# An fp32 attention layer with a gated residual: the last head group's order of TensorE, ScalarE and VectorE work, and a result formed in two parts

## The reference

```python
xn = layernorm(x)
q, k, v = xn @ Wq.T, xn @ Wk.T, xn @ Wv.T       # 32, 8 and 8 heads of 128
q, k = rmsnorm(q, q_norm_w), rmsnorm(k, k_norm_w)
attn = softmax(q @ k.T / sqrt(128) + alibi_bias)  # causal, a slope for each head
s = (attn @ v) @ Wo.T
z = xn @ W.T + bias + sum_n(coef_n * (xn @ A_n.T) @ B_n.T)
out = x + s * (z * sigmoid(z))                    # x + s * silu(z)
```

## Time and profile before

| | us |
|---|---|
| median of 3 runs | 2694.29 |
| lowest, highest | 2690.87, 2695.27 |
| the profiled execution | 2691.18 |
| its span, first to last instruction | 2689.4 |
| TensorE busy in it | 2591.1 |
| GpSimd busy in it | 1705.5 |

### The profile page before, as it was taken

One profiled execution on the slowest core, in us unless ns is written; L12 is line 12 of the kernel. 1 busy time (PEld: TensorE's weight loads), 2 busy tenths in 40 slices (PEclk: granted clock), 3 DMA queues, 4 the chain that ended last, 5 costly groups with the idle time before them and its releaser, 6 DMA issues.

```text
span 2689.4 us, 39881 instructions
## 1 busy us (share of the span) xinstructions
PE 2591.1 (96%) x13840; PEld 2297.7 (85%) x13840; DVE 1648.2 (61%) x3530; ACT 1771.1 (66%) x4635; POOL 1705.5 (63%) x835
## 2 busy tenths in 40 slices
PE   5689999999999999999999999999999999999997
PEld 4578888888888888888888888888888888888886
DVE  6446566657667556566566666556666755655666
ACT  4366666666776667667767667666767666666763
POOL 3377877876667656656667656565666756655653
PEclk9899999999999999999999999999999999999999
DMA  7888788775445333433335433433334533333323
GB/s 259 269 269 281 240 266 263 256 259 190 128 145 174 109 119 100 154 111 104 110 106 183 133 117 104 154 105 106 112 108 136 180 110 106 118 110 118 111 69 129
DMA packets 179192, 418.45 MB, mean 156 GB/s; under 512 B 31152, under 2 KB 72240, under 8 KB 178096
## 3 DMA queue, kind: packets, MB, share of 16 engines
q1 hardware_dynamic: 177728, 414.78, 47.4%
q10 hardware_dynamic: 1264, 1.12, 0.1%
HBM read 343.48 MB, written 89.13 MB: 161 GB/s over the span
## 4 chain that ended last, share of the span: by engine, by line
PE 89%; DVE 3%; ACT 2%; DMA 2%; POOL 1%; issue 1%; SPq 1%; POOLq 0%; DVEq 0%; ACTq 0%
PE proj L486 21%; PE proj L488 21%; PE proj L487 21%; PE tr L581 5%; PE sc L486 3%; PE sc L487 3%; PE sc L488 3%; PE ot L487 3%; PE tr L561 3%; PE ot L488 3%; PE ot L486 3%; PE tr L554 1%; DMA wu<-xtok 1%; SPq L313 1%; DVE acc L1226 1%
## 5 line engine op out<-in xcount | busy, mean ns | idle before, releaser
L985 POOL TENSOR_TENSOR wl<-wl,wh 128x896 fp32r<-128x896 f32 x436 | 948.9, 2206 | 608.7 <-ACT wh L740 608.6
L486 PE MATMUL proj<-wh,xh 128*128 128x448 f32 x1792 | 673.8, 376 | 25.0 <-POOL wl L985 17.5
L487 PE MATMUL proj<-wl,xh 128*128 128x448 f32 x1792 | 661.1, 369 | 0.0
L488 PE MATMUL proj<-wh,xl 128*128 128x448 f32 x1792 | 661.1, 369 | 0.0
L996 POOL TENSOR_TENSOR wb_lo<-wb_lo,wb_hi 128x1024 fp32r<-128x1024 f32 x128 | 307.2, 2400 | 315.6 <-ACT wb_hi L750 315.6
L807 ACT ACTIVATE misc<-misc,negmax 128x128 f32<-128x128 f32 (+3 forms) x512 | 286.8, 565 | 250.2 <-DVE negmax L1202 250.2
L486 PE MATMUL proj<-o_hi,wb_hi 128*128 128x512 f32 x1024 | 424.9, 415 | 9.3 <-issue 6.1
L1226 DVE TENSOR_TENSOR acc<-acc,proj 128x512 f32<-128x512 f32 x480 | 327.7, 684 | 156.6 <-PE proj L488 155.3
L786 ACT ACTIVATE pT_hi<-tr 128x512 fp32r<-128x512 f32 (+3 forms) x512 | 197.3, 440 | 334.5 <-PE tr L581 334.5
L740 ACT ACTIVATE wh<-wl 128x896 fp32r<-128x896 f32 x436 | 395.5, 966 | 33.0 <-DMA wl<-wu 32.5
L488 PE MATMUL proj<-o_hi,wb_lo 128*128 128x512 f32 x1024 | 404.6, 395 | 0.0
(11 more groups left out here) (125 smaller groups left out, 4366.6 us busy)
## 6 DMA issues: line engine op xcount, KB each, us to landing
wl<-wu SPq DMA_DIRECT2D x436, 448.0 KB, 3.9
wb_lo<-wo_in SPq DMA_DIRECT2D x128, 512.0 KB, 3.3
wu<-xtok SPq DMA_DIRECT2D x13, 1792.0 KB, 10.2
wo_in<-wo SPq DMA_DIRECT2D x32, 512.0 KB, 6.0
xtok<-wa SPq DMA_DIRECT2D x52, 256.0 KB, 4.6
wu<-xtok SPq DMA_DIRECT2D x13, 896.0 KB, 5.6
gate_dram<-misc SPq DMA_DIRECT2D x32, 256.0 KB, 5.1
xtok<-xT SPq DMA_DIRECT2D x28, 256.0 KB, 5.1
```

Of the source, the lines that this page charges most:

```text
L486: pe.matmul(out, hi_l, hi_r, start=first, stop=False, skip_group_check=onto)
L487: pe.matmul(out, hi_l, lo_r, start=False, stop=False, skip_group_check=onto)
L488: return pe.matmul(out, lo_l, hi_r, start=False, stop=last, skip_group_check=onto)
L985: pool.tensor_tensor(w_slot(wl, w), w_slot(wl, w, True), w_slot(wh, w), ALU.subtract).then_inc(w_ready, 1)
```

## The change

Everything concerns the last group (n = 31) and what follows it.

- TensorE: for even v, `out_first` issues the first head's six matmuls (c = 0 into one bank, c = 1 into the other) before it waits for the second head, then the second head's six.
- ScalarE: `normalise` comes ahead of the copies of the turned queries, `split_b` behind three `probs_hi`.
- VectorE: `last_part` puts `add_out(v, 0)` first, and gives two of the four reciprocals to j = 0 and two to j = 1, one before and one behind the three `probs_lo`.
- GpSimd: `values_lo` ahead of `low_b` at j = 0.
- The result for c = 4 to 7: in the last step, once v = 125 is added, `base` forms acc x gate on VectorE and `add_base` adds it to x on GpSimd. After v = 127, `last_result` multiplies the bank of PSUM itself with the gate, with no `add_out`, and `finish` adds. The store of the gate and the loads of the second half come two steps earlier in SyncE's queue.

The core of the diff:

```diff
                         load_result(b, 0)
+                        store_gate(n)
+                        load_result(b, 1)
...
                     load_product(n + 2, P1)
                     load_product(n + 2, P2)
-                    store_gate(n)
+                    if n + 1 < NG:
+                        store_gate(n)
...
 
+            def out_head(v, c, hh, bank):
+                pair = v % 4 // 2
+                w = slice(hh * 512 + c * P, hh * 512 + c * P + P)
+                return three(bank[:], wb_hi[:, v % 2, w], wb_lo[:, v % 2, w],
+                             o_hi[:, pair, hh, :], o_lo[:, pair, hh, :], hh == 0, hh == 1)
...
+                out_head(v, c, 1, bank).then_inc(out_done, 1)
+
+            def out_first(v):
+
+                pe.wait_ge(wb_ready, v + 1)
+                pe.wait_ge(ot_free, v // 2 * 2 + 1)
+                banks = []
+                for c in range(2):
+                    banks.append(proj_bank(("o", v, c)))
+                    out_head(v, c, 0, banks[c])
+                pe.wait_ge(ot_free, v // 2 * 2 + 2)
+                for c in range(2):
+                    out_head(v, c, 1, banks[c]).then_inc(out_done, 1)
...
+                if n + 1 == NG and v % 2 == 0:
+                    out_first(v)
+                elif v >= 0:
...
-            for v in (NV - 2, NV - 1):
-                out_ready(v)
-                for c in range(4):
-                    out_proj(v, c)
+            out_first(NV - 2)
+            for c in range(2, 4):
+                out_proj(NV - 2, c)
+            out_ready(NV - 1)
+            for c in range(4):
+                out_proj(NV - 1, c)
...
                 if m > 0:
                     head_out(m - 1)
+                if last:
+                    normalise(m)
                 if j == 0:
                     queries_hi(n, 1)
                 if j == 1:
                     queries_hi(n, 2)
                     queries_hi(n, 3)
-                if j == 3 and n + 1 < NG:
+                if j == 3 and not last:
                     keys_hi(n + 1)
                     queries_hi(n + 1, 0)
-                normalise(m)
+                if not last:
+                    normalise(m)
                 if j == 0:
                     gate_in(n)
-                else:
+                elif not last:
                     split_b(v + 1)
                 pieces, fills = unit_pieces(n, j), x_fills(n, j)
...
                 split_product(*[(n + 1, P6), (n + 1, P4), (n + 1, P3), (n + 2, P1)][j])
+                if last:
+                    split_b(v + 1)
...
+                if j == 0 and n + 1 == NG:
+                    values_lo(n)
                 low_b(v + 1)
...
                     low_product(*[(n + 1, P7), (n + 1, P5), None, (n + 2, P2)][j])
+                if j == 3 and n + 1 == NG:
+                    for c in range(4, NK):
+                        add_base(c)
+
+            def add_base(c):
+
+                x = result_slots(BATCH - 1, c)[0]
+                pool.wait_ge(base_step, c - 3)
+                pool.tensor_tensor(x, x, acc[:, c, :], ALU.add).then_inc(base_done, 1)
 
             def finish(b, half):
                 for c in range(4 * half, 4 * half + 4):
                     x, gate = result_slots(b, c)
+                    if b + 1 == BATCH and half == 1:
+                        pool.wait_ge(base_done, c - 3)
                     pool.wait_ge(fin_step, b * NK + c + 1)
                     pool.tensor_tensor(x, x, gate, ALU.add).then_inc(fin_done, 1)
 
...
                 dve.tensor_tensor(gate, gate, acc[:, c, :], ALU.mult).then_inc(fin_step, 1)
+
+            def base(c):
+
+                dve.wait_ge(out_free, 4 * (NV - 3) + c % 4 + 1)
+                dve.wait_ge(fin_last[c % 4], 32)
+                dve.tensor_tensor(acc[:, c, :], acc[:, c, :], result_slots(BATCH - 1, c)[1], ALU.mult
+                                  ).then_inc(base_step, 1)
+
+            def last_result(c):
+
+                gate = result_slots(BATCH - 1, c)[1]
+                bank = proj_ps[PJ["o", NV - 1, c % 4] % 2][:]
+                dve.wait_ge(base_step, c - 3)
+                dve.wait_ge(out_done, 4 * (NV - 1) + c % 4 + 1)
+                dve.tensor_tensor(gate, gate, bank, ALU.mult).then_inc(fin_step, 1)
 
             def weight_sum(g, h, p):
                 b11, b12, b21, b22 = (prep_tile(g, h, a, c) for a in range(2) for c in range(2))
...
 
+            def last_part(n, j):
+
+                m, v = 4 * n + j, 4 * n + j - 2
+                add_out(v, 0)
+                if j == 0:
+                    queries_lo(n, 1)
+                    gate_sum(n)
+                if j == 1:
+                    queries_lo(n, 2)
+                    queries_lo(n, 3)
+                if j == 3:
+                    base(4)
+                add_out(v, 1)
+                if j < 2:
+                    gate_inverse(n, 2 * j)
+                if j == 3:
+                    base(5)
+                for k in range(3):
+                    probs_lo(m, k)
+                if j < 2:
+                    gate_inverse(n, 2 * j + 1)
+                if j == 1:
+                    gate_product(n)
+                add_out(v, 2)
+                probs_lo(m, 3)
+                if j == 3:
+                    base(6)
+                add_out(v, 3)
+                if j == 3:
+                    base(7)
+
             for n in range(NG):
                 for j in range(G):
                     step(n, j)
             head_out(NH - 1)
-            for half in range(2):
-                for c in range(4):
-                    add_out(NV - 2 + half, c)
-                    result(BATCH - 1, 4 * half + c)
+            for c in range(4):
+                add_out(NV - 2, c)
+                result(BATCH - 1, c)
```

More of the change, by code:

```diff
@@ L181, in build_layer @@
         fin_in = [sem(f"fin_in{i}") for i in range(4)]
+        fin_last = [sem(f"fin_last{i}") for i in range(4)]
         res_out = [sem(f"res_out{i}") for i in range(4)]
@@ L367, in load_result @@
                         need(sp, res_out[c % 4], 16 * (2 * b + half))
-                    sp.dma_start(x, xT[b * NK + c]).then_inc(fin_in[c % 4], 16)
-                    sp.dma_start(gate, gate_dram[b % 2 * NK + c]).then_inc(fin_in[c % 4], 16)
+                    landed = fin_last if b + 1 == BATCH and half == 1 else fin_in
+                    sp.dma_start(x, xT[b * NK + c]).then_inc(landed[c % 4], 16)
+                    sp.dma_start(gate, gate_dram[b % 2 * NK + c]).then_inc(landed[c % 4], 16)
             def store_result(b, half):
@@ L609, in out_ready @@
                 pe.wait_ge(ot_free, v // 2 * 2 + 2)
+            def out_head(v, c, hh, bank):
[3 more added lines that the diff above has]
+                             o_hi[:, pair, hh, :], o_lo[:, pair, hh, :], hh == 0, hh == 1)
             def out_proj(v, c):
                 bank = proj_bank(("o", v, c))
[L613 to L618, removed]
+                out_head(v, c, 0, bank)
+                out_head(v, c, 1, bank).then_inc(out_done, 1)
[9 more added lines that the diff above has]
+                    out_head(v, c, 1, banks[c]).then_inc(out_done, 1)
             def merge_gate(half, k):
@@ L935, in step @@
                         values_hi(n)
-                if j == 0 and n + 1 == NG:
+                if j == 0 and last:
                     gate_exp_of(n)
-                    split_b(v + 1)
                     values_hi(n)
@@ L1071, in step @@
                     x_sum(next_x, P6)
-                if j == 0:
+                if j == 0 and n + 1 < NG:
                     values_lo(n)
@@ L1348, in step @@
                     head_out(m - 1)
-                if j == 0:
+                if j == 0 and more:
                     queries_lo(n, 1)
-                if j == 1:
+                if j == 1 and more:
                     queries_lo(n, 2)
@@ L1362, in step @@
                         weight_sums(1, 1)
+                if not more:
+                    last_part(n, j)
+                    return
                 late_gate = g == 7 and next_x
@@ L1385, in step @@
                         scale_rows("q1")
-                if j == 0 and not more:
-                    gate_sum(n)
-                if j == 0 and not late_gate:
+                if j == 0 and more and not late_gate:
                     for quarter in range(4):
```

15 lines of the change are left out of this document (9 added, 6 removed).

## The result

The changed kernel takes 2686.30 us (median of nine runs, 2682.22 to 2689.95) beside 2693.54 us for the kernel before (nine runs, 2690.87 to 2695.27): a ratio of 0.9974, 95% interval 0.9964 to 0.9984, 7.2 us less. A second comparison later (e9) gave 0.9983, 0.9974 to 0.9992.

A forecast was written before the change was run, and what follows sets the result against it. TensorE was taken to bound the kernel, with last-group gaps and low clock, then GpSimd the end. Gains of 4.2 us up to head 127 and 0.7 in the tail made 4.9: 2694.3 - 4.9 = 2689.4 us, range 2685.5 to 2693.

The forecast's parts named there:

- the steps up to head 127: Heads 124 to 127: 3.3 us gained after head 124, 2.5 left after 125, 4.2 at the turns of head 127.
- The wait ahead of the third score product of head 126: TensorE in head 126: waits 1.6 us there instead of 0.4, for VectorE's gate product ending at 2636.24.
- scaling first gains nothing: Head 125, ScalarE: scaling ready 1.0 us earlier, but turns need the query banks, copied behind scaling; nothing gained.
- rival 2: TensorE's clock falls behind a wait of 1.6 or 1.5 us: 1.4 lost, 3.5 gained, 2690.8 us; chance 0.18.
- GpSimd and VectorE in turns: VectorE's two-SBUF operations alternate with GpSimd's, ending 0.54 to 0.55 us after them; six such turns reckoned at 3.3 us.
- The loads: SyncE, block 4: x and gate land by 2651.9 us, wanted at 2655.8, so 3.9 us to spare.
- rival 3: Block 4's loads land late and stop VectorE at `base(4)`; some 2700 us if landing at 2666; chance 0.05 with similar losses.
- the tail: After head 127's turns: 0.7 us more gained, on top of 4.2, from a tail that could have given 3 to 4.
- GpSimd becomes the bound, and I count it: End of kernel: GpSimd runs without gap from 2659.2 for 22.7 us (4.7 + 14.7 + 3.3), ending at 2681.9.
- Rival 1: GpSimd is not held by turns with VectorE: 4.9 to 7.7 us gained, some 2687; chance 0.17.
- I carry the gain over to the median of three: Gain reckoned on the profiled execution of 2691.18 us, applied to median 2694.29: 2694.3 - 4.9 = 2689.4 us.

The follow-up runs named there:

- e9: The changed kernel once more, no edit, against the kernel before: 2684.04 us, ratio 0.9983 (0.9974 to 0.9992), stretch 69.95 us.
- e4: Changed kernel with GpSimd's additions of blocks 4 and 5 moved ahead of `wb_lo` of v = 126: ratio to the kernel before 0.9978, stretch 69.18 us.
- e3: Changed kernel with ScalarE's old order (scaling behind the queries, `split_b` ahead of the probability copies): ratio to the kernel before 0.9969, stretch 67.37 us.
- e8: Changed kernel with only `split_b` back ahead of the probability copies, scaling left first: ratio to the kernel before 0.9977, stretch 67.95 us.
- e2: Changed kernel with the first-head matmuls put back behind the wait for both heads: ratio to the kernel before 0.9987, stretch 73.77 us.
- e1: The kernel before once more, no edit, for a second profile: ratio 1.0004 (0.9995 to 1.0012), stretch 77.93 us.
- e5: Changed kernel with the four reciprocals together again ahead of the first sum: ratio to the kernel before 0.9989, stretch 72.35 us.
- e11: Changed kernel, ScalarE's old order, all eight blocks formed ahead, early additions of blocks 2 and 3 behind `wb_lo` of v = 126: ratio to kernel before 0.9969.
- e10: Changed kernel, ScalarE's old order, all eight blocks formed ahead, early additions of blocks 0 to 3 ahead of `wb_lo` of v = 126: ratio to kernel before 0.9967.

## Why the prediction was right, and where it was not

**Right: the steps up to head 127.** Counted from head 124's eight turns, the next scores come 3.3 sooner in head 124 and 2.5 sooner in 125, head 127's turns 4.2, as forecast (13.09 to 9.77, 25.71 to 23.21, 48.79 to 44.57 us). The wait ahead of the third score product of head 126 is 1.37 where 1.6 was given. The turns of the queries wait for their banks, so scaling first gains nothing. The waits of 1.37 and 1.29 that are left kept the clock, and rival 2's own mechanism did not happen in either profile of the changed kernel.

**Right: GpSimd and VectorE in turns.** The gate's product ends at 2636.55, 0.55 after GpSimd's operation, `base(6)` again 0.55. The page "SBUF — State Buffer" of the Trainium skill (SBUF: two separate sides) calls their port pair an exclusive lock; the trace agrees. It also shows what stays outside: the L1305 products with a PSUM input took 0.69 beside running additions. The loads had room and rival 3 had nothing in it.

**Mis-sized: the tail.** It gave 1.0 (5.2 less 4.2) where 0.7 was reckoned. GpSimd's chain took 22.29 for 22.7: with its own work at the 4.7 and 14.7 of the sum, 2.9 are left for the turns, where six at 0.55 (3.3) were put. (The addition between turns is 1.19 by its own figures, (6.39 - 1.65) / 4, not 1.17; that moves the sum by 0.1.)

**Wrong reading: "GpSimd becomes the bound, and I count it".** The end was right and the reason half right. A chain without gaps suggests that each operation taken out shortens it. e4 took out two additions ahead, some 2.5 us, and 0.7 came off: only 0.7 behind GpSimd's own work stands the alternation, 1.91 a block. The prediction had the other side ready with three additions to spare (VectorE's last product near 2677.4) and TensorE released by `wb_lo` of v = 127. That operation ended at 2670.68, near the 2670.8 forecast, but TensorE started v = 127 at 2671.98, behind a sum of VectorE, which its own products held up; VectorE's last product ended at 2679.07. Rival 1 (7.7 gained if the turns were free) counts GpSimd's own work alone, too.

**Missed: the cost of ScalarE's order.** The prediction put the split later, reckoned GpSimd's start from it, and found the gate's product meeting `wb_lo`; it never asked what the stretch would be without that edit. e3 and e8 show it: 1.9 us for the late split and 0.6 for the query order, a third of what the change could have given. The parts, by leaving one out of the changed kernel: first head early 3.9, reciprocals spread 2.5, half the result ahead 1.1, ScalarE's order -2.5. They add up to 5.0 beside the measured 5.2, which is no proof, since parts that act on each other need not add up. They are read from stretches, of one profile each (ScalarE's order from two); the device times do not tell e2 to e8 from the changed kernel, as their intervals overlap. The early loads and `values_lo` ahead of `low_b` are in every variant of the changed kernel and were not tried alone.

**Where the number was off: the carry to the median.** The time forecast was 2689.4 and 2686.3 was measured: inside the range, but 7.2 gained for 4.9, just beyond the 0.2% that I held likelier not to be reached. The interval of that gain is 4.3 to 9.7 us, so 4.9 is inside it and the excess may be chance. If it is real, the step is "I carry the gain over to the median of three", and beside it rival 2's "other executions of the kernel before pay less than the profiled one for the low clock". e1 shows one that pays 2.9 more, the other way. Spreading the reciprocals takes away the wait behind which the clock fell (3.21 in e1, 4.06 in e5), and with it not only the stall but a risk of 3 us. By stretches the gain is 5.2 against the first profile and 8.1 against e1. How often the kernel before falls into each is not known from two profiles, and the second comparison gave 4.3 us of gain; so e1 can account for the larger figure, and is not proved to be its cause.

**The clock.** Behind waits of 3.21, 3.23 and 4.06 us the granted clock was low, behind 1.61 (first profile) and less full. Behind 1.86 it was 0.55 in one execution of the kernel before and full in the other and in e2; behind 2.76 it was 0.50 all three times (first profile, e1, e2). Behind 1.95 (e11) and 2.32 (e10) it was full, behind 2.35 (e2) 0.50. So in these runs the length of a wait alone does not decide between 1.86 and 2.35; what does, no run here shows. The page "TensorE: Matmul & The Clock Gate" of the Trainium skill (Why this matters for your kernels) asks for no gap over about 3 us: the three longest agree, and so do the 1.95 and 2.32 that kept it; the 2.76 and 2.35 do not, nor does the 1.86 of the earlier trace rows.

## What to carry to other kernels

A change in several parts deserves a reckoning of each part without the others: here one of four cost 2.5 us while the forecast of the whole looked right to a third of a us. Two engines that take turns are a single resource: count their operations together, keep the operations of one out of the other's critical stretch, and let the last product read PSUM where it can. Where a stall may lower TensorE's clock (here behind 1.86 us in one of three executions), one profile gives one draw of its price; profile the unchanged kernel twice before carrying a gain of a few us to a median.

## What had not been expected of the hardware

The same wait of 1.86 us, in the same program, led to a clock of 0.55 once and 1.00 once, and with it the low clock moved to another wait and the stretch from 75.05 to 77.93 us. A wait of 2.32 us left the clock full in e10, one of 2.35 halved it in e2. VectorE and GpSimd, both with work queued, each ran one 512-column operation in turn: an addition of 1.28 and a gap of 0.63, which in the tail made an operation of 0.7 last 1.28 on VectorE.
